# Gathering the routed experts' results and their layer norm inside the pipeline of the second attention

## The reference, cut to what matters

```python
def _layernorm(x, axis=-1, eps=1e-05):
    m = jnp.mean(x, axis=axis, keepdims=True)
    v = jnp.var(x, axis=axis, keepdims=True)
    return (x - m) / jnp.sqrt(v + eps)
...
    combine = (jax.nn.one_hot(indices, E, dtype=weights.dtype) * weights[..., None]).sum(axis=1)
    y = jnp.zeros_like(xt)
    for e in range(E):
        y = y + _mlp(xt, w1[e], w2[e], w3[e]) * combine[:, e:e + 1]
    z = _mlp(xt, sw1, sw2, sw3)
    return (y + z).reshape(shape)
...
    x = x + jnp.tanh(g_xattn[0]) * _L0_xattn_ref(_layernorm(x, axis=-1), ctx_1024, ...)
    x = x + jnp.tanh(g_ffn[0]) * _L0_ffn_ref(_layernorm(x, axis=-1), ...)
    x = x + jnp.tanh(g_xattn[1]) * _L1_xattn_ref(_layernorm(x, axis=-1), ctx_1024, ...)
    x = x + jnp.tanh(g_ffn[1]) * _L1_ffn_ref(_layernorm(x, axis=-1), ...)
```

## Time and profile before

| | us |
|---|---|
| median of 3 runs (2535.66 to 2539.21) | 2537.47 |
| the profiled execution: its time | 2542.62 |
| the profiled execution: its span, first to last instruction | 2540.9 |
| first attention | 50 to 700 |
| weights of the experts, router, routing, shared expert | 700 to 1070 |
| routed experts | 1070 to 1407 |
| combine, weight split, layer norm: until the attention's first normalising | 1407 to 1531 |
| second attention's pipeline | 1531 to 2313 |
| last block | 2313 to 2541 |

### The profile page before, as it was taken

The page is one execution under the profiler, slowest core; times in us unless marked ns, Lnnn a source line. Parts: engine busy times, 40 slices in busy tenths (PEclk is TensorE's granted clock), DMA queues, the critical chain, the costliest instruction groups (busy, mean ns, idle before and its releaser), DMA issues. The chain is left out here.

```text
span 2540.9 us, 49106 instructions
## 1 busy us (share of the span) xinstructions
PE 1907.3 (75%) x14719; PEld 1378.0 (54%) x14728; DVE 1617.6 (64%) x4016; ACT 1126.6 (44%) x2555; POOL 831.7 (33%) x1334
## 2 busy tenths in 40 slices
PE   1798898998804795299999008999989989993367
PEld 1576676676503463166666006777777767772123
DVE  5777777777466542144444454777677777777696
ACT  1354454554443121022222105767767767763463
POOL 2000000000000233322221656667667667661004
PEclk9799999999955898699999659999999999997595
DMA  3000000000062000011111423223223323311001
GB/s 100 9 5 8 8 4 8 8 4 4 1 214 76 1 0 1 22 56 56 56 56 48 139 69 92 68 54 75 72 50 75 75 50 75 75 42 35 0 0 67
DMA packets 91393, 117.77 MB, mean 46 GB/s; under 512 B 18200, under 2 KB 60840, under 8 KB 91304
## 3 DMA queue, kind: packets, MB, share of 16 engines
q1 hardware_dynamic: 82728, 98.93, 14.2%
q0 software_dynamic: 8576, 17.87, 2.5%
HBM read 56.92 MB, written 17.90 MB: 29 GB/s over the span
## 5 line engine op out<-in xcount | busy, mean ns | idle before, releaser
L912 POOL TENSOR_SCALAR a_P<-a_P,a_RS 128x256 f32<-128x256 f32 x512 | 249.2, 487 | 184.0 <-DVE a_RS L1152 150.5
L1077 ACT ACTIVATE a_P<-a_P,a_NM 128x256 f32<-128x256 f32 x512 | 255.7, 502 | 118.3 <-DVE a_NM L1146 117.6
L1146 DVE CUSTOM_DVE_ANT_0 a_P<-a_pS,a_maskq 128x256 f32<-128x256 f32 x512 | 195.2, 419 | 88.1 <-PE a_pS L993 71.7
L504 PE MATMUL a_pT<-a_Q,a_K 128*128 128x256 f32 x1024 | 243.5, 384 | 8.7 <-ACT a_PT L587 8.7
L587 ACT ACTIVATE a_PT<-a_pT 128x512 f32<-128x512 f32 x256 | 151.3, 597 | 187.9 <-PE a_pT L504 187.5
L504 PEld LDWEIGHTS a_pT<-a_Q,a_K 128*128 128x128 f32 x1024 | 183.7, 191 | 39.2 <-ACT a_PT L587 16.6
L1158 DVE TENSOR_TENSOR a_PL<-a_pT,a_PH 128x512 f16<-128x512 f32 x256 | 173.8, 679 | 36.1 <-ACT a_PH L1086 32.6
L420 POOL TENSOR_TENSOR a_cl<-a_ctxin,a_ch 128x512 f16<-128x512 f32 x16 | 18.5, 1159 | 543.1 <-ACT a_ch L557 543.1
L1086 ACT ACTIVATE a_PH<-a_pT 128x512 f16<-128x512 f32 x256 | 151.5, 592 | 87.2 <-PE a_pT L1001 83.3
L694 DVE TENSOR_REDUCE a_M<-a_pS 128x2 f32<-128x512 f32 x256 | 163.0, 683 | 32.7 <-PE a_pS L483 32.1
L1001 PE MATMUL a_pT<-g_ident,a_P 128*128 128x128 f32 x1024 | 157.6, 277 | 15.4 <-POOL a_P L912 15.3
(11 more groups left out here) (410 smaller groups left out, 5679.8 us busy)
## 6 DMA issues: line engine op xcount, KB each, us to landing
a_KD<-a_KN SPq DMA_DIRECT2D x128, 128.0 KB, 2.4
a_QS<-a_QN SPq DMA_DIRECT2D x128, 128.0 KB, 2.3
we_stage<-mw SPq DMA_DIRECT2D x24, 512.0 KB, 4.5
ys<-me_yb SPq DMA_DIRECT2D x72, 128.0 KB, 1.7
a_ctxin<-ctxT SPq DMA_DIRECT2D x32, 256.0 KB, 2.7
a_KZ<-a_KN SPq DMA_DIRECT2D x64, 128.0 KB, 2.4
g_X<-x SPq DMA_DIRECT2D x1, 4096.0 KB, 14.8
rows<-mr_row SPq DMA_DIRECT2D x32, 128.0 KB, 1.7
```

Of the source, the lines that this page charges most:

```text
L504: last = nc.tensor.matmul(pT[h % 2][:, kt, :], K32[par][h % 2][:, h // 2, kt * P:(kt + 1) * P], Q32[par][:, h // 2, :], start=True, stop=True)
L912: last = nc.gpsimd.tensor_scalar(P32[u % 4][:, a, :], P32[u % 4][:, a, :], RS[u % 4][:, a:a + 1], LIFT, ALU.mult, ALU.mult)
L1077: last = nc.scalar.activation(P32[u % 4][:, a, :], P32[u % 4][:, a, :], ACT.Exp, bias=NM[u % 4][:, a:a + 1], scale=-1.0, accum_out=SM[u % ...
L1146: last = nc.vector.tensor_tensor_reduce(P32[u % 4][:, a, :], pS[u % 2][:, a, :], maskq[par][:, u % 2, :], 1.0, 3.0e38, ALU.add, ALU.min, N ...
```

## The change

- The combine stage and the layer norm's stage (`moe_combine`, `layernorm_stats` "l2") are gone. Their work is a third plan, `comb`, which runs two steps ahead of the batch that needs it. GpSimd, turn 8: four index copies and four gathers. VectorE, turn 12: four additions, two tile statistics, two aggregations, variance plus epsilon. GpSimd, turn 13: power -0.5 of two columns. VectorE, turn 15: four small steps of one refinement of the reciprocal root. `comb` stands last in its turn. Batch 0's is done alone before the pipeline, batch 1's beside the first front, those of batches 2 to 15 in 14 full steps.
- `KZ` is cleared on GpSimd, at the start of the attention's stage.
- The weights of the second attention are loaded and split during the routed experts, in eight parts of 128x1024: loads issued by ScalarE, high parts on ScalarE, low parts on GpSimd. The loops over the 72 steps are cut into nine for these two engines. The parts lie in `XW`, which shares its memory with the router's `XT`.
- The tile `pF` of job n now alternates with the batch's parity too. The transposes of x wait for all but the last of the earlier values, and the first keys wait for the last.
- The hardware loop of the attention has six passes in place of seven; more steps are written out around it.

```diff
-def moe_combine(nc, ctx, X, st, POS, GW, y_d):
...
-    def batches(eng, front, back):
+    def batches(eng, comb, front, back):
...
+        run(UNITS, comb(0, 0, 0))
+        run(UNITS, now(front(0, 0)), comb(1, 1, 0))
+        step(back(0, 0), idle, later(front(0, 0)), now(front(1, 1)), comb(2, 0, 1))
+        with eng.Fori(0, B // 2 - 2) as i:
+            b = i * 2 + 1
+            step(back(b, 1), back(b - 1, 0), later(front(b, 1)), now(front(b + 1, 0)), comb(b + 2, 1, i + 1))
+            step(back(b + 1, 0), back(b, 1), later(front(b + 1, 0)), now(front(b + 2, 1)), comb(b + 3, 0, i + 2))
...
+    GATHER, ADD, ROOT, REFINE = 8, 12, 13, 15
...
+            for z in (z for zs in KZ for z in zs):
+                nc.gpsimd.memset(z[64:P, :, :], 0.0).then_inc(cleared, 1)
...
+                def gathers():
...
+                    for q in range(2 * TOPK):
+                        nc.gpsimd.tensor_copy(pick[par][q][:], POS[:, q % TOPK, bass.ds(2 * b + q // TOPK, 1)]).then_inc(pick_ready.sem, 1)
+                    pick_ready.wait(pool, b, 4)
+                    nc.gpsimd.nop(nofuse=True)
+                    for q in range(2 * TOPK):
+                        nc.gpsimd.indirect_dma_start(out=routed[par][q][:], out_offset=None, in_=y_d,
+                                                     in_offset=bass.IndirectOffsetOnAxis(ap=pick[par][q][:], axis=0)).then_inc(gathered[par].sem, 16)
+
+                def inverse_root():
+                    var_ready.wait(pool, b, 1)
+                    nc.gpsimd.nop(nofuse=True)
+                    nc.gpsimd.tensor_tensor(root[:], var[:], half[:], ALU.pow).then_inc(root_ready.sem, 1)
+                return plan((GATHER, gathers), (ROOT, inverse_root))
...
                 def inputs():
                     xn_ready.wait(pe, b, 1)
-                    v_lo.wait(pe, b, 0)
+                    if not isinstance(b, int) or b:
+                        v_lo.wait(pe, b, -1)
...
                         if q == 0:
                             ctx_lo.wait(pe, b, 1)
+                            v_lo.wait(pe, b, 0)
...
+                def add():
+                    comb_steps.begin(b)
+                    gathered[par].wait(dve, turn, 64)
+                    for k in range(TOPK):
+                        for j in range(2):
+                            x = X[:, bass.ds(2 * b + j, 1), :].rearrange("p a d -> p (a d)")
+                            last = nc.vector.scalar_tensor_tensor(x, routed[par][TOPK * j + k][:], GW[:, k, bass.ds(2 * b + j, 1)], x, ALU.mult, ALU.add)
+                        link(last)
+                    nc.vector.nop(nofuse=True)
+                    for j in range(2):
+                        last = nc.vector.bn_stats(bn[:, j, :], X[:, bass.ds(2 * b + j, 1), :].rearrange("p a d -> p (a d)"))
+                    last.then_inc(combined.sem, 1)
+                    combined.wait(dve, b, 1)
...
+                return plan((ADD, add), (REFINE, finish))
...
+                def next_low(j):
+                    pool.wait_ge(next_hi, j + 1)
+                    nc.gpsimd.tensor_tensor(columns(j, 1), stage[j % 2][:], columns(j, 0), ALU.subtract).then_inc(next_lo, 1)
...
+            def next_high(j):
+                if j >= 1 and j + 1 < AHEAD:
+                    act.wait_ge(next_lo, j)
+                    next_load(nc.scalar, j + 1)
+                act.wait_ge(staged[j % 2], 16 * (j // 2 + 1))
+                nc.scalar.activation(columns(j, 0), stage[j % 2][:], ACT.Copy).then_inc(next_hi, 1)
```

More of the change, by code:

```diff
@@ L781, in attention1 @@
     proj = s.sb("proj", [P, 2, D])
+    pick = [[s.sb(f"pick{i}{q}", [P, 1], U32) for q in range(2 * TOPK)] for i in range(2)]
+    routed = [[s.sb(f"routed{i}{q}", [P, D]) for q in range(2 * TOPK)] for i in range(2)]
+    bn = s.sb("bn", [P, 2, 6])
+    moments = [s.sb(f"moments{i}", [P, 2, 2]) for i in range(2)]
+    rstd = [s.sb(f"rstd{i}", [P, 2]) for i in range(2)]
+    half, var, root, corr = s.sb("half", [P, 2]), s.sb("var", [P, 2]), s.sb("root", [P, 2]), s.sb("corr", [P, 2])
     pF = [s.ps(f"pF{i}", [P, 512]) for i in range(2)]
@@ L793, in attention1 @@
     f_full = s.counter("f_full", 13)
+    pick_ready, gathered = s.counter("pick_ready", 4), [s.counter(f"gathered{i}", 64, start=0) for i in range(2)]
+    combined, var_ready, root_ready = s.counter("combined", 1), s.counter("var_ready", 1), s.counter("root_ready", 1)
+    comb_steps = s.chain("comb_steps", 7)
     k_flat, q_flat = s.counter("k_flat", 4), s.counter("q_flat", 4)
@@ L1094, in back @@
                         plan(*[(u, lambda u=u: exps(u)) for u in range(UNITS)]))
-            batches(act, front, back)
+            batches(act, uncombined, front, back)
         @block.vector
```

178 lines of the change are left out of this document (91 added, 87 removed).

## The result

The changed kernel takes 2563.59 us (median of 4 runs, 2562.59 to 2568.45), the kernel before 2536.56 us (4 runs, 2534.32 to 2539.21): 1.011 times as long, 95% interval 1.0092 to 1.0127. In a later session with 5 rounds it was 1.0117 (1.0096 to 1.0138). So the change makes the kernel slower by 27 us, as forecast, at somewhat more than half of the price: the prediction was 2583 us, 45.6 us over the kernel before.

The account below looks back on a forecast made before the run. TensorE sets the attention's pace, with GpSimd just as full in turns 8 to 12. Terms: -101.6 + 8 + 14 x 10.3 - 4 - 2 + 1 = +45.6 on 2537.5, so 2583 us; range 2505 to 2625.

Parts of the forecast that it names:

- 6.3 us a step: Full steps, turn 8: copies and gathers delay GpSimd's normalising of unit 8 and TensorE behind it; +6.3 us, lower bound 5.3.
- Rival (b): Full steps: GpSimd catches up behind the gathers, a step costs 3 us or less; 2481 us or lower, chance 0.08.
- rival (a): Full steps: VectorE's additions run in idle time, a step costs less than 7.0 us, kernel faster; chance 0.17.
- Rival (d): Gathers issue slower beside VectorE, 8 us a batch, not 6.3: 2607 us; chance beyond the forecast 0.14 together with (c).
- Rival (c): Full steps: clock or lock in full, +14 us a step, 2635 us; chance beyond the forecast 0.14 together with (d).
- VectorE's term: Full steps, additions in turn 12 and refinement in 15: about +4 us a step, bounds +1 and +6.
- the 8.6 us of the prediction: Turn 12: length of VectorE's additions if each of the four waits for a GpSimd operation of up to 1.15 us.
- The first front: Batch 1's gathers ahead of the sixth split and VectorE's additions ahead of the first maximum: +8 us (6 to 11).
- The rule for `pF`: Transposes of x may run within TensorE's wait for the last values: -0.3 us a batch, -4 in all (-15 to 0).
- The end of the stage: Attention's hardware loop: one loop's end fewer, -2 us.
- The stage that went: Combine stage gone: first normalising at 1429.5 in place of 1531.1 us, a gain of 101.6 us.
- the weight split: Routed experts: ScalarE hides its copies and DMA issues in idle time ahead of the SiLU; +1 us (0 to 8).

Follow-up runs that it names:

- e1: The changed kernel without the index copies and gathers of batches 2 to 15 on GpSimd; VectorE still adds: 50.05 us a step, 6.30 shorter.
- e3: The changed kernel with all its work, the next batch's copies and gathers spread over turns 13 to 1 in place of turn 8: 50.01 us a step.
- e2: The changed kernel without VectorE's additions, statistics and refinement of batches 2 to 15; GpSimd's copies, gathers and root stay: 54.29 us a step, 2.06 shorter.
- e11: The changed kernel with the edits of e1 and e2, and without GpSimd's root of batches 2 to 15: 47.46 us a step.
- e6: The changed kernel with the edits of e3 and e4, VectorE's additions taken apart into turns 9 and 11: 0.12 us a step less than e3.
- e4: The changed kernel with KZ cleared on VectorE and batches 0 and 1 gathered at once at the stage's start: 1.0062 of the time before.
- e9: e6 with its loop over 2 batches made one over 4, three passes for six: 0.9671 of the time before.

## Why the prediction was right, and where its terms were off

**The direction and the mechanism were right.** 64 gathers left a stage where TensorE idled, and 56 of them went to a place where GpSimd had nothing to spare. The forecast rested on two rows, the split that is followed by the normalising 0.10 us later, and the transposes that wait 0.45 us for the next one. It said 6.3 us a step for this; e1 shows 6.30 and e3 that it is the place. Rival (b), that GpSimd's fullness is only apparent, falls with that. So does rival (a) in its form: it needed VectorE's additions under 0.7 us, and they cost 2.06. Rival (d) is out as well: the four copies and gathers of a step take 6.2 us, not 8. Rival (c), 14 us a step, is out by the total: VectorE does wait for GpSimd in turn 12, as it says, but for 0.7 us and not for 6 (see below). The clock did fall: the transposes behind the wait take 1.12 us in place of 0.60, and from 1825 to 2260 us the mean granted clock (the sixth figure) was 0.98 before and is

```profile
1825.00:2260.00 435.00, 353.56 (x3000) 268.49 (x2998) 303.37 (x1019) 260.23 (x777) 291.70 (x452) 0.94 0.26 65
```

But e3, which does the same work and is back at 0.97 from 1600 to 2100 us, wins no more than the 6.3 us that GpSimd's instructions take. The rows of turns 11 and 12 show how. Behind the wait of 5.08 us the granted clock is at its lower level, 1.2 GHz:

```profile
1719.00:1722.00 3.00, 2.87 (x14) 2.22 (x14) 0.69 (x1) 1.57 (x5) 2.68 (x5) 0.50 0.06 23
```

TensorE takes 3.04 us from the transposes of unit 8 to those of unit 9 (1719.13 to 1722.17), where before it took 2.14, the wait of 0.45 in it. But GpSimd's normalising of unit 9 ends at 1721.08 + 1.03 = 1722.11, so at full clock TensorE would have waited until then. In this step the lower clock fills a wait that was there anyway. In e2 the clock is lower still:

```profile
1600.00:2100.00 500.00, 426.88 (x3626) 329.74 (x3623) 326.03 (x1103) 312.98 (x935) 349.51 (x542) 0.91 0.27 68
```

So the 0.53 us that e11 frees beyond the two single parts may also be this clock; clock, root or shared waiting stays open.

The price came out as forecast in kind, but at the lower end: 2563.6 us in 2558 to 2607, and 8.9 us a step by e11 in 8.5 to 12.

**VectorE's term was too large: 4 where 2.06 is measured.** The step that failed is the length of the block in turn 12, 5.7 us where 4.0 is measured, and both of its parts were too large. Undisturbed it takes 3.3 us and not 4.0: batch 0's instructions, with GpSimd idle beside the additions, take 3.29 us from the first addition to the end of the variance (1422.15 to 1425.44), and the 1.07 us for two additions in the earlier trace rows hold about 0.1 us of idle time between them. And what GpSimd adds beside it is 0.7 us and not 1.7: 0.22 us in each of two additions, and the variance takes 0.50 us beside a subtraction in place of 0.17. That 1.7 was taken from the pair that normalises x, which starts just behind a GpSimd operation of 1.15 us; in turn 12 GpSimd normalises, and of its shorter instructions only what is left of each has to be waited for. The second addition of the first pair, and GpSimd's instruction beside it:

```profile
1724.67 0.58 POOL L942 TENSOR_SCALAR a_P<-a_P,a_RS 128x256 f32<-128x256 f32 x1
...
1724.82 0.70 DVE L1149 SCALAR_TENSOR_TENSOR g_X<-a_routed,g_GW,g_X 128x256 f32 x1
```

GpSimd's ends at 1725.25, the addition at 1725.52, 0.27 us later, as in e6. In the 11 traces that keep the additions, 295 of the 704 take 0.47 to 0.49 us; the other 409 are longer, and every one of them ends 0.27 to 0.29 us behind the end of a GpSimd normalising, cast or subtraction. For a VectorE instruction with two SBUF inputs and a GpSimd one that reads SBUF, the Trainium skill (SBUF — State Buffer, section "SBUF: two separate sides") calls the pair of ports that they share an exclusive lock, which the one that starts first holds for its whole length while the other fully blocks. This case's traces agree: all 409 end as if they had waited for the whole of GpSimd's instruction. What the 8.6 us of the prediction had wrong is how many of the four additions have to wait and for how long: in turn 12 two of them, 0.22 us each.

With 4.0 us in place of 5.7 the prediction's own working gives 1.8 us in a step without a loop's end and 3.1 in one with it; 1.5 and 2.8 are measured. The difference of 1.3 between the two kinds of step is the one it gave (3.5 and 4.8). It put that down to a loop's end that absorbs nothing of the refinement; VectorE's idle time there also grew by about 1 us, which it did not foresee, so the agreement may be luck.

**Small terms.** The first front costs 10.9 us in place of 8, at the upper end of the 6 to 11 given: e4 shows 7.2 for the gathers and leaves 3.7 for VectorE, whose four additions stand beside GpSimd's splits there and take 4.2 us, not 1.8. The rule for `pF` is worth 0.50 us a step and not 0.3; the prediction saw that the keys stand behind the transposes with a wait of their own, and took too little of the 0.66 us of the transposes as won. The end of the stage is 4.0 us shorter, 2 forecast: a loop end costs 2.5 by e9, the other 1.5 were not taken apart, and in the other kernels the same stretch takes 83.1 to 85.7 us. The stage that went is right to 1 us, and that is partly luck. The 7.0 us of clearing, 6.1 of copies and gathers and 2.8 to the landing are as worked out, and the stage began 1.9 us earlier than assumed, which lies within the movement of its start. But from the landing to the first normalising it takes 6.3 us and not 5.2: the additions are 0.7 us shorter than forecast, the root and the refinement 1.9 us longer (3.1 us, 1.2 forecast). The routed experts end 1.9 us earlier than before, and ScalarE's idle time ahead of the SiLU is 144.4 us, 155.8 before: the weight split costs nothing there that the profile shows. The runs of the experiments begin the stage anywhere within 12 us, so 1.9 us is no gain either.

**The sum.** It was 24.7 us too high against the profiled spans (18.6 against the medians), 22.6 of them in the full steps (140.2 against 117.6). There VectorE's term was 14 x 1.94 = 27 us too high and that of `pF` 3; about 7 of it come back as the 0.53 us a step that neither of the two engines' parts shows when it is left out alone. The other stretches leave 2: 2.0 at the start, 2.0 in the stage's last batch and 1.0 behind it, less 2.9 in the first front.

## What to carry to other kernels

Work that goes from a stage of its own into a pipeline costs what it costs in the turn where it stands: the same eight GpSimd instructions cost 6.3 us a step in turn 8, 1.2 as a block in turn 14, and nothing that can be measured when taken apart over turns 13 to 1. So find, in the timeline of the engine that gets the work, the turns whose rows have idle brackets ahead of them, and not the turn in which the result is wanted; here a block put between two rows without a bracket, with another engine's wait behind them, had a price of its full length. Read the costs of a pipeline from distances between the same instruction in successive steps, which here repeated to 0.2 us in 789 for one kernel (and to 2.3 in 700 for two with the same step) while the starts moved by 12. And when work goes beside another engine that it can be held up by, look at how long that engine's single instructions are: the same additions took 1.80, 2.19 and 3.55 us for four, beside nothing, beside scalings of 0.5 us and beside subtractions of 1.2 us.

## What the runs showed of the hardware

- A VectorE addition with two tensors in SBUF waits for the end of the GpSimd instruction that it falls behind, be it one with two tensor inputs or with one. Alone it takes 0.48 us; held up, it ends 0.27 to 0.29 us behind GpSimd's (409 additions in 11 traces). Two of them take 1.78 us where a subtraction of 1.16 us is in the way (e6) and 1.09 us beside scalings of 0.5 to 0.6 us; the pair that normalises x takes 1.59 us beside the subtraction and 0.73 alone.
- Four index copies and four indirect gathers occupy GpSimd for 6.2 us, of which the wait for the copies' end is 0.80 and each gather 1.25 (0.95 and 0.30 of idle). A power on two columns took 0.73 us on GpSimd.
- Clearing 64x2048 float16 takes 1.76 us on GpSimd (7.02 for four) and 0.91 on VectorE (e4), where the trace lists it as 64x1024 uint32.
- A loop's end costs about 2.5 us a pass in this pipeline (e9). VectorE's first maximum behind it has idle time of 2.2 to 2.8 us in the kernels without VectorE's new part and of 3.3 to 3.7 in those with it and the loop over 2 batches; in most of these rows the engine waited for nothing that the profile shows, as in the changed kernel:

```profile
1740.19 0.42 DVE L1211 CUSTOM_DVE_ANT_0 a_P<-a_pS,a_maskq 128x256 f32<-128x256 f32 x1 [3.47 <-issue]
```
